# Key phase, two projections and the output phase of a four-layer graph network: a clear between two scatters, sums taken before the moments, and the last phase written out

## What is computed

```python
h = jnp.maximum(_layernorm(x, axis=-1), 0.0)
x = x + _L0_gnn_ref(h, edge_index, ...)   # 3 rounds of attention, x += sigmoid(gat(x)) in each
h = jnp.maximum(_layernorm(x, axis=-1), 0.0)
x = x + _L1_gnn_ref(h, deg_isqrt, src, dst, edge_type_100, ...)   # relational, 4 bases, 100 types
h = jnp.maximum(_layernorm(x, axis=-1), 0.0)
x = x + _L2_gnn_ref(h, edge_index, ...)   # attention with 8 heads
h = jnp.maximum(_layernorm(x, axis=-1), 0.0)
x = x + _L3_gnn_ref(h, edge_index, ...)   # edge features
# in the last layer, for the output phase below:
#   s = (h + seg_sum) / maximum(cnt, 1);  z = concat(features, s) @ W_lin.T + b_lin
```

## Time and profile before

| | |
|---|---|
| time, 3 runs | 3926.29, 3939.06, 3943.65 us (median 3939.06) |
| profiled execution | 3923.35 us, span 3921.4 us |
| PE busy | 2263.7 us, 58% |
| DVE busy | 2282.0 us, 58% |
| ACT busy | 1610.7 us, 41% |
| POOL busy | 2157.8 us, 55% |

### The profile page before, as it was taken

One profiled execution on the slowest core, in us unless ns is written; L12 is line 12 of the kernel. 1 busy time (PEld: TensorE's weight loads), 2 busy tenths in 40 slices (PEclk: granted clock), 3 DMA queues, 4 the chain that ended last, 5 costly groups with the idle time before them and its releaser, 6 DMA issues. The chain is left out here.

```text
span 3921.4 us, 53964 instructions
## 1 busy us (share of the span) xinstructions
PE 2263.7 (58%) x12833; PEld 1777.4 (45%) x12833; DVE 2282.0 (58%) x8009; ACT 1610.7 (41%) x3565; POOL 2157.8 (55%) x2121
## 2 busy tenths in 40 slices
PE   1035899999898565465565567754526443344333
PEld 1023676676677554364464444434425332233222
DVE  4154999999898785334345378866575333333233
ACT  0005999999997573223323322324411222122100
POOL 3618765575564332581185255546500588888755
PEclk9998999999999786577577588887756666666665
DMA  2140122332231454651663733333304333333253
GB/s 64 27 181 20 44 90 87 100 103 87 87 92 39 133 157 116 161 139 42 186 174 87 203 95 99 87 98 81 90 16 118 109 74 64 75 74 65 51 145 117
DMA packets 569029, 380.48 MB, mean 97 GB/s; under 512 B 51389, under 2 KB 511942, under 8 KB 568386
## 3 DMA queue, kind: packets, MB, share of 16 engines
q1 hardware_dynamic: 510050, 329.99, 28.7%
q0 software_dynamic: 56000, 46.29, 6.4%
q10 hardware_dynamic: 2720, 1.23, 0.2%
HBM read 249.08 MB, written 153.32 MB: 103 GB/s over the span
## 5 line engine op out<-in xcount | busy, mean ns | idle before, releaser
L1309 POOL DMA_INDIRECT p_a<-t_d,k_map_ix x300 | 309.1, 1030 | 291.3 <-DMA p_a<-t_d 241.1
L807 POOL TENSOR_TENSOR a_rs<-a_ve,w_neg_half 128x16 f32<-128x16 f32 x113 | 330.1, 2922 | 241.7 <-DVE a_ve L743 227.7
L833 ACT ACTIVATE a_nr<-a_xb,a_nm,a_rs 128x128 f32<-128x128 f32 x882 | 369.9, 487 | 26.1 <-POOL a_nm L809 26.1
L2064 POOL DMA_INDIRECT e_a<-t_d,e_ix x200 | 210.4, 1052 | 277.1 <-DMA e_a<-t_s 219.2
L895 PE MATMUL a_ps<-w_ident,a_nr 128*128 128x128 f32 x1568 | 245.6, 280 | 128.8 <-DVE a_xb L754 47.3
L903 PE MATMUL a_ps<-a_ht,w_aug 128*128 128x512 f32 x588 | 312.7, 616 | 2.4 <-DVE a_ht L710 2.4
L895 PEld LDWEIGHTS a_ps<-w_ident,a_nr 128*128 128x128 f32 x1568 | 179.9, 143 | 277.0 <-issue 244.5
L1431 PE MATMUL p_pm<-w_aug,p_ht 128*128 128x130 f32 (+1 forms) x1600 | 277.1, 343 | 7.6 <-ACT p_ht L1392 3.8
L710 DVE TENSOR_TENSOR a_ht<-a_ps,a_ht 128x512 f32<-128x512 f32 x294 | 201.5, 686 | 134.7 <-ACT a_ps L848 111.0
L1431 PEld LDWEIGHTS p_pm<-w_aug,p_ht 128*128 128x128 f32 x1600 | 261.4, 250 | 21.4 <-ACT p_ht L1392 11.9
L1789 PE MATMUL c_pq<-layer_src,c_sel 128*128 (+1 forms) x800 | 194.3, 420 | 124.7 <-ACT c_sel L1760 72.2
(11 more groups left out here) (358 smaller groups left out, 6449.0 us busy)
## 6 DMA issues: line engine op xcount, KB each, us to landing
t_s<-p_a SPq DMA_DIRECT2D x100, 256.0 KB
c_a<-t_d SPq DMA_DIRECT2D x100, 256.0 KB
t_d<-c_a SPq DMA_DIRECT2D x100, 256.0 KB
a_xa<-in_x SPq DMA_DIRECT2D x98, 256.0 KB
out<-a_xb SPq DMA_DIRECT2D x98, 256.0 KB, 2.0
p_a<-t_s SPq DMA_DIRECT2D x75, 256.0 KB
p_a<-t_d SPq DMA_DIRECT2D x75, 256.0 KB
t_acc<-q_zt SPq DMA_DIRECT2D x3, 2171.5 KB
```

The source lines that it names most:

```text
L807: nc.gpsimd.tensor_tensor(RS[:, z, :], VE[:, z, :], w["neg_half"][:, None, 0:J].to_broadcast([P, LNS, J]), ALU.pow).then_inc(s_rstd.sem, 1)
L833: last = nc.scalar.activation(NR[k][:, T.at(NORM[k], 2), cols(j)], normed_rows(T, k)[:, cols(j)], ACT.Identity, bias=NM[:, T.at(1, SHORT), ...
L1309: eng.indirect_dma_start(out=A[:, g, SRC, j, :], out_offset=None, in_=t[f"d{r}"], in_offset=bass.IndirectOffsetOnAxis(ap=k["map_ix"][:, b ...
L2064: eng.indirect_dma_start(out=A[:, g, side, j, :], out_offset=None, in_=t[f"d{r}"], in_offset=bass.IndirectOffsetOnAxis(ap=IX[:, g, what, j ...
```

## The change

Three edits. In `keys` each scatter is followed by a clear of 128x256 floats on POOL, as in `project`. In `project` DVE's order within a turn is changed for the kinds with a norm: the moments come last, and for "normed" `residual` follows `hold` at the same lag of 3. In `edge_outputs` all 25 blocks are written out, the scatters read their indices in place, the rings are 8 deep, and each scatter is followed by a clear.

```diff
@@ keys, POOL
             for c in range(T):
                 eng.indirect_dma_start(out=t["maps"], ... in_=ID[:, c:c + 1], ...).then_inc(s_map1, 16)
+                if c:
+                    eng.wait_ge(s_idle, c)
+                nc.gpsimd.memset(IDLE[:, :], 0.0).then_inc(s_idle, 1)
@@ project, DVE
-            holds, residuals = (3, 4) if norm else (0, 1)
+            holds = 3 if norm else 0
+            residuals = holds if normed else holds + 1
             for n in range(BLOCKS + residuals):
+                if not normed and 0 <= n - residuals:
+                    residual(n - residuals)
+                if 0 <= n - holds < BLOCKS:
+                    hold(n - holds)
+                if normed and 0 <= n - residuals:
+                    residual(n - residuals)
                 if norm and n <= BLOCKS:
                     if n < BLOCKS:
                         there(eng, n)
                     mo.turn(eng, lambda m: A[:, n % RING, m // J, m % J, :], n, BLOCKS - 1)
-                if 0 <= n - residuals:
-                    residual(n - residuals)
-                if 0 <= n - holds < BLOCKS:
-                    hold(n - holds)
@@ edge_outputs
+    RING, BANKS = 8, 2
@@ SP
-                wait(eng, s_out[g], (b // GE) * (16 * J))
-                carry_waits(eng, w)
+                if b >= RING:
+                    eng.wait_ge(s_out[g], (uses(b) - 1) * (16 * J))
@@ POOL
+            for b in range(BLOCKS):
+                g = b % RING
+                eng.wait_ge(s_out_in, b + 1)
                 for j in range(J):
-                    eng.indirect_dma_start(out=out, out_offset=bass.IndirectOffsetOnAxis(ap=IX[:, g, j:j + 1], axis=0),
+                    m = b * J + j
+                    eng.indirect_dma_start(out=out, out_offset=bass.IndirectOffsetOnAxis(ap=k["out_s_ix"][:, m:m + 1], axis=0),
+                    if m:
+                        eng.wait_ge(s_idle, m)
+                    nc.gpsimd.memset(IDLE[:, :], 0.0).then_inc(s_idle, 1)
@@ DVE
-                v.tensor_scalar(IX[:, g, :], tiles_of(k["out_s_ix"], b), 0.0, None, ALU.add).then_inc(s_ix, 1)
-            stream(eng, (count_, 0), (finish, 1), (summed, 0))
+            for n in range(BLOCKS + 1):
+                if n < BLOCKS:
+                    summed(n)
+                if n:
+                    finish(n - 1)
@@ PE
-            stream(eng, (turn, 0), (product, 0))
+            for n in range(BLOCKS + 1):
+                if n < BLOCKS:
+                    turn(n)
+                if n:
+                    product(n - 1)
```

More of the change, by code:

```diff
@@ L221, in keys @@
         M1 = sb("m1", [P, T], I32)
+        IDLE, s_idle = sb("idle", [P, 256]), sem("idle")
         OF = sb("of", [T, 2, P])
@@ L2239, in edge_outputs @@
         sem = lambda n: ctx.semaphore("o_" + n)
[L2240 to L2248, removed]
@@ L2249, in edge_outputs @@
-        s_load = [sem(f"load{g}") for g in range(GE)]
-        s_out = [sem(f"out{g}") for g in range(GE)]
+        ACC = sb("acc", [P, RING, J, M])
+        GT = sb("gt", [P, RING, J * C])
+        SZ = sb("sz", [P, RING, J, C])
+        UP = sb("up", [P, RING, J, C])
+        CN = sb("cn", [P, RING, J, 1])
+        IDLE = sb("idle", [P, 256])
+        PT = [ctx.enter_context(nc.psum_tensor(f"o_pt{n}", [P, J, C], F32)) for n in range(BANKS)]
+        PM = [ctx.enter_context(nc.psum_tensor(f"o_pm{n}", [P, J, C], F32)) for n in range(BANKS)]
@@ L2251, in edge_outputs @@
+        s_cnt, s_tp, s_s, s_mm, s_up, s_out_in, s_idle = (sem(n) for n in "cnt tp s mm up out_in idle".split())
+        s_load, s_out = ([sem(f"{n}{g}") for g in range(RING)] for n in ("load", "out"))
         block = ctx.enter_context(nc.Block())
-        before = lambda b, g: b - (1 if g == 0 else 2)
+        uses = lambda b: b // RING + 1
         @block.sync
         def _(eng):
-            def load(b, g):
-                wait(eng, s_out[g], (b // GE) * (16 * J))
-                carry_waits(eng, w)
+            for b in range(BLOCKS):
+                g = b % RING
+                if b >= RING:
+                    eng.wait_ge(s_out[g], (uses(b) - 1) * (16 * J))
@@ L2260, in load @@
                 eng.dma_start(ACC[:, g, :, :], block_rows(t["acc"], b)).then_inc(s_load[g], 16)
-                eng.dma_start(GT[:, g, :], t["gt"][bass.ds(number(b) * P, P), :]).then_inc(s_load[g], 16)
+                eng.dma_start(GT[:, g, :], t["gt"][b * P:(b + 1) * P, :]).then_inc(s_load[g], 16)
                 eng.dma_start(SZ[:, g, :, :], block_rows(t["sz"], b)).then_inc(s_load[g], 16)
-            stream(eng, (load, 0))
         @block.gpsimd
         def _(eng):
[L2268 to L2271, removed]
+            for b in range(BLOCKS):
+                g = b % RING
+                eng.wait_ge(s_out_in, b + 1)
@@ L2278, in _ @@
-            for g in range(GE):
-                eng.wait_ge(s_out[g], 16 * J * ROUNDS_E)
+                    if m:
+                        eng.wait_ge(s_idle, m)
+                    nc.gpsimd.memset(IDLE[:, :], 0.0).then_inc(s_idle, 1)
+            for g in range(RING):
+                eng.wait_ge(s_out[g], 16 * J * len(range(g, BLOCKS, RING)))
         @block.vector
@@ L2307, in _, with turn @@
+            for n in range(BLOCKS + 1):
[3 more added lines that the diff above has]
+                    finish(n - 1)
         @block.tensor
         def _(eng):
-            def turn(b, g):
-                wait(eng, s_load[g], (b // GE + 1) * 48)
-                wait(eng, s_s, before(b, g) + 1)
+            def turn(b):
+                g = b % RING
+                eng.wait_ge(s_load[g], uses(b) * 48)
+                if b >= BANKS:
+                    eng.wait_ge(s_s, b - BANKS + 1)
@@ L2312, in turn, with product @@
                 for j in range(J):
-                    last = nc.tensor.transpose(PT[g % 2][:, j, :], ACC[:, g, j, 0:C], w["ident"][:, :])
+                    last = nc.tensor.transpose(PT[b % BANKS][:, j, :], ACC[:, g, j, 0:C], w["ident"][:, :])
                 last.then_inc(s_tp, 1)
-            def product(b, g):
-                wait(eng, s_s, b + 1)
-                wait(eng, s_up, before(b, g) + 1)
+            def product(b):
+                g = b % RING
+                eng.wait_ge(s_s, b + 1)
+                if b >= BANKS:
+                    eng.wait_ge(s_up, b - BANKS + 1)
@@ L2319, in product @@
                 for j in range(J):
-                    last = nc.tensor.matmul(PM[g % 2][:, j, :], GT[:, g, j * C:(j + 1) * C], w["wlT"][:, 1, :], start=True, stop=True)
+                    last = nc.tensor.matmul(PM[b % BANKS][:, j, :], GT[:, g, j * C:(j + 1) * C], w["wlT"][:, 1, :], start=True, stop=True)
                 last.then_inc(s_mm, 1)
-            stream(eng, (turn, 0), (product, 0))
+            for n in range(BLOCKS + 1):
[3 more added lines that the diff above has]
+                    product(n - 1)
```

26 lines of the change are left out of this document (12 added, 14 removed).

## The result

Median of four runs 4087.87 us (4084.68 to 4093.5), against 3940.16 for the kernel before (3926.29 to 3943.65, four runs, one taken beside the new ones): 1.038 times the time before, interval 1.036 to 1.041. Slower, by 148 us; 4078 had been forecast.

A forecast was written before the change was run, and what follows sets the result against it. No engine fills the span: scatter-time stalls of DVE bound the key phase, DVE is fullest in round 0. +122 + 86 - 54 - 4 = +150 on 3923.35 makes 4073, said as 4078; range 4020 to 4125.

The forecast's parts named there:

- The order, round 0: Round 0 projection: kept sums ahead of moments make chain and moments add up each turn, +122 us (96 to 131).
- two sizes with three of four long: Projections: PE's sixteen products take 3.79 or 2.21 us; three of four turns assumed long, giving round 0 turns of 10.83.
- the idle time before L1350: Sign in the projections: DVE idles before L1350 for the products of L1438, some 3 to 5 us a turn.
- the same chain: Projections: DVE's shift, ACT's scaling and copy, PE's products, then DVE's kept sum; 7.54 us from shift to sum in round 0.
- The order, "normed": "Normed" projection: the same exposed chain, turns of 12.12 us in place of 8.49, +86 us (+53 to +97).
- the wait for gathers vanishes behind the chain: "Normed" projection: DVE's 86.3 us wait for gathered rows disappears, gathers with clears needing 6.0 us a block.
- The clears of the key phase: Key phase: scatters with clears start 1.494 us apart and DVE's loop is let go, next phase at 216.7, -54 us.
- The step that had been called an inference: Key phase: POOL's queue, in a long unbroken run of scatters, causes DVE's stalls, and clears relieve it.
- The +16: Key phase: cost in us if clears do not relieve the stalls and POOL needs 20 us longer; kept for the range.
- The output phase: Output phase: clears fill POOL's idle time, scatters 1.494 us apart, 3917.8 against 3921.4, -4 us.
- The hidden chain: Rival, chance 0.06: DVE waits for nothing, projections keep their time, 3870 us; 55 less, 3815, if "normed" gains from sooner slots.
- the rival that stalls are no matter of POOL's queue: Rival, chance 0.08: taken branches in loops cause the stalls, so the key phase keeps them, +16 for -54, 4148 us.

The follow-up runs named there:

- e11: Changed kernel with only ACT's order in the projections made to follow DVE's new order, PE's order left: 4081.3 us, one run.
- e5: The kernel before, unedited, profiled again on another occasion: 3845.4 us, one run.
- e6: The changed kernel, unedited, run again beside e5: 4082.2 us, 1.061 times the kernel before.
- e7: Changed kernel with DVE's old order, moments first, keeping only the "normed" row sum's shorter lag and all clears: 3828.0 us, 0.996 of the kernel before.
- e2: Changed kernel, DVE's new order kept, with ACT's and PE's orders in the projections with a norm made to follow: 3814.4 us, 0.995 of the kernel before.
- e12: e2 with clears of 16 columns in place of 256, third run, on an occasion with stalls: 3870.4 us, 0.980 of the kernel before.
- e9: Kernel before with only the three orders of e2 (DVE, ACT, PE), no clears added: 3779.8 us, 0.984 of the kernel before.
- e8: e2 with clears of 16 columns in place of 256, first run: 3781.0 us, 0.983 of the kernel before.
- e10: Same kernel as e8, second run, beside e9: 3782.4 us, 0.985 of the kernel before.

## Why the prediction was right, and where it was not

**The order, round 0: +122 predicted, +127.7 measured.** Mechanism and pieces are as told. The turns were 11.04 us on average in place of 10.83: (1522.5 - 1264.8) less the first two intervals, 3.1 and 11.7, leaves 242.9 for 22. The products were not of two sizes with three of four long, as I had assumed: over the turns that wait they took 2.5 to 3.7 us, 3.07 on average, where the assumption makes 2.80 of it (3.20 less a quarter of 1.58, a difference that I had taken from the other projection's products). That accounts for the 0.2 us a turn. The size lies inside the bounds, 96 to 131. One place was named wrongly. I expected the idle time before L1350; most of it stands before L1363, 4.74 us in the turn shown, because ACT's sigmoid is queued behind the same scaling and copy. It lies under the same chain and costs nothing of its own: in e11, where the sigmoid leaves that queue, the wait moves to L1350 (5.50) and the phase stays at 282.

**The order, "normed": +86 predicted, +83.5 measured.** The shifts run from 2738.2 to 3018.3, 11.7 a turn over all 24 intervals. In the steady part turns of 12.5 and 11.4 alternate, with products of 3.8 and 2.7: the long size was right, but it came in one of two turns and not in three of four, and the other size lay above my 2.21. That the wait for gathers vanishes behind the chain is right: 86.3 became 18.2. Beside e5 the difference was +73.4 (e6), since the kernel before had there 245.3 in place of 233.5. What e7 adds is that this part of the change, taken without the rest, is a gain.

**The clears of the key phase: -54 predicted, -51.1 measured, and right only where stalls are.** The period was 1.53 in place of 1.494, so the last scatter started at 209.2 and not at 205.3; the 10.4 us behind it came out exactly. The step that had been called an inference, that the clears relieve the stalls, held in the trace of the changed kernel. But the trace of one execution had been taken for the program. On three other occasions the stalls were absent and this term is +20.1, the output phase's +19.2 in place of -2.8. The forecast of 4078 stands in both, 4087.9 and 4082.2, since it is the kernel before that moves; the forecast slowdown, 4078 against 3939, does not hold without stalls. That the result was taken on an occasion of the kind that the trace had shown was luck, for nothing in the prediction asked whether the stalls are always there. The +16 that I had kept in case the clears relieve nothing is the nearest that the prediction had to this.

**The output phase: -4 predicted, -2.8 measured**, as a sum of POOL's clears and the stalls that they take away. This too holds only with stalls.

**The rivals.** The hidden chain did not occur in the changed kernel, but e2 built it with two more orders: round 0 took what it takes in the kernel before, and "normed" 65 us less than in e5, where the rival had put 55. Beside the rival that stalls are no matter of POOL's queue stood a rule of the Trainium skill ("Runtime: NRT & Kernel Launch", section "Instruction fetch mechanics"): a taken branch whose target is outside the window forces a fetch. The runs decide against branches as the cause: e5 has all the loops and no stall, e12 stalls in an output phase that has none, and in the kernel before it is the product's signal that comes late, with no more instruction packets than in e5. Nor is the unbroken run of scatters alone enough, for e5 has it too. What is shown is a condition of the occasion, together with scatters that follow each other closely. The condition does not go with the chip alone: under number 9 the record has both e5 to e11, without stalls, and e12. What brings the condition is open, and so is why the signals are late, and whether it is the pause or the clear itself that relieves them between 0.14 and 0.34 us; no kernel here puts a pause of another kind between two scatters.

## What to carry to other kernels

In a pipeline over three engines with queues in order, an instruction moved ahead on one engine is only early if the queues that feed it are reordered in the same way: here one and the same order of DVE costs 211 us with the others left as they were, and gives 62 us with both made to follow. The following takes the loss away; it is not what brings the gain, since round 0 ends where it began (155.6 against 156.0 in e9 and e5) and in "normed" the slot freed one turn sooner gives most of the 65 us by itself (e7). Count in turns how long a ring's slot is held; one turn less was worth 48 to 56 us. And profile the kernel before on more than one occasion before paying for a remedy: clears and output phase together gave 54 us where the stalls were, and cost 39 us where they were not. Without stalls e9 and the kernel of e8 and e10 are the fastest run here, and level with each other; with stalls that same kernel was 78 us under the kernel before (e12). e2, whose long clears should relieve the stalls as they did in the changed kernel, was not run there.

## What the runs showed of the hardware that was not expected

The kernel before took 3820 to 3855 us on three occasions and 3926 to 3954 on two, with nothing between. The traces put this down to the two phases in which POOL scatters without a pause, 72.2 and 22.2 us, less the 11.8 by which the "normed" projection was shorter in the execution with stalls. The granted clock went with the orders: a mean of 0.65 in round 0 of the changed kernel, where PE is busy for 126 of 282 us, against 0.83 in e2, 95 of 155 us with the same instructions. And a semaphore raised by PE can reach DVE late by up to 18.6 us while POOL scatters without a pause; the same program shows 0.02 on another occasion.
